# A hand-set order for the five engines of an attention stage, set anew, with 28 changes of array tiling per batch in place of 29

## The chip, the cores and the metric

One Trainium2 chip, one of its cores. The metric is device time in microseconds (us) of one launch, the median of three runs. Times and waits come from one profiled execution of the kernel before. Engines are called as in the profile: PE is TensorE, DVE is VectorE, ACT is ScalarE, POOL is GpSimd, SP is the sync engine, which here only starts DMAs.

## What is computed

The input is 32 sequences (batches) of 256 tokens with 128 features. Two layers are applied, each as `x = x + attention(norm(x)) * silu(ffn(norm(x)))`. Cut to what matters:

```python
x = L0_attn_x                                   # 32 x 256 x 128
xn = _layernorm(x)
s = _L0_attn_ref(xn, ...)                       # a recurrence over the tokens
g = _silu(_L0_ffn_ref(xn, ...))                 # eight experts, one per token
x = x + s * g
xn = _layernorm(x)                              # from here: the last stage
s = _L1_attn_ref(xn, ...)                       # 16 heads of 8, keys in blocks of 64
g = _silu(_L1_ffn_ref(xn, ...))                 # 4 of 16 heads of 64, chosen per batch
return x + s * g
```

`_L1_attn_ref` is a softmax attention whose maximum and correction go block by block over the keys. `_L1_ffn_ref` computes router logits per batch, takes the four best of 16 heads, runs a softmax attention over those and projects the result.

## The kernel before

**Stages.** The first stages (normalization, the recurrence, the experts with their scatter and gather through memory) end at about 398 us. The change is in the last stage alone. It treats one batch at a time, all of its 256 tokens, and is written out without a loop on the chip: `run(eng, step)` calls `step` 36 times (32 batches and four more) for each engine, and a step works on up to five batches at once. `lag(quad, p, k)` gives the batch that came in k steps ago, so `batch0` is the newest and `batch4` the oldest; `runs` leaves a part out where there is no such batch.

```python
            for t in range(B + 4):
                step(t // NQ, t % NQ)
```

**What sets the order.** Nothing but the lines of the five `step` functions. Each engine works through its own list in that order, one instruction after the other. Between engines there are semaphores: `wait_ge(s, n)` waits until s has counted n, `then_inc(s, 1)` counts when an instruction is done, `after(...)` is a wait that is left out while its count is zero or less. A late signal therefore holds back everything that stands behind the waiting instruction on its engine.

**PSUM.** The eight banks are shared out by hand:

```python
        bS, bT = banks[:, 0:1024], banks[:, 1024:2048]
        bC, bA, bF1, bF2 = PS[4], PS[5], PS[6], PS[7]
        bF, bR = (bF1, bF2), (bS, bT)
```

`bS` holds one group of scores at a time, and `bT` one group of shifted scores; both also take the chosen heads' scores (`bR`). `bC` holds P times V, `bA` is used in turn by the transposed input, the logits, both projections and the attention's own output, `bF1` and `bF2` by the chosen heads and the transposed outputs.

**The parts of a batch and their lines** (numbers of the kernel before; those of PE stand 7 higher in the changed kernel, ACT 5, DVE 3, POOL 1).

- PE: `transpose_x` L1858, `logits` L1864, `project_qk` L1869, `project_v` L1876, `transpose_max` L1886, `scores` 0 to 7 L1898, `shifted_scores` 0 to 7 L1912, `values` 0 to 3 L1922, `transpose_o` 0 to 3 L1936, `transpose_attn` L1945, `project_out` L1952, `head_qk` 0 and 1 L1963, `head_v` L1970, `head_scores` 0 and 1 L1983, `head_pt` 0 to 3 L1997, `head_out` 0 and 1 L2005, `routed_out` L2012 and L2014.
- DVE: `ln_stats` L1505, `route_a` L1516 to L1522 (with the heads' indices), `route_b` L1529, `route_c` L1536 and L1542, `qk_rest` L1549, `head_qk` L1557, `block_max` 0 to 7 L1565, `row_max` L1575, `head_max` L1585, `head_pt` L1592, `attn_norm` L1609 to L1616, `final` L1624.
- ACT: `xT_copy` L1696, `qk_copy` L1701, `probs` L1705 and L1706, `gate_exps` L1710, `mT_copy` L1721, `head_qk` L1732, `head_exp` L1747, `head_pt` L1755, `head_ot` L1761, `routed_tanh` L1767, `exp_scores` 0 to 7 L1773, `ot_copy` 0 to 3 L1778, `attnT_copy` L1783.
- POOL: `gather` L1372 and L1376 (two indirect DMAs for the rows of one batch, from batch 2 on), `inverse_std` L1388, `ln_apply` L1394, `minus_top` L1400, `minus_inverse` L1404, `head_biases` L1409, `split` L1417 and L1418, `split_max` L1425 to L1434, `finish` L1442 and L1445, `head_norm` L1451 and L1454.
- SP: `store_max` L1319 writes the row maxima to memory and `load_max` L1324 reads them back as three more rows of `QS`, which `shifted_scores` 0 waits for; `load_qk` L1313, `load_heads` L1335, `store_parts` L1300, `load_biases` L1342, `store_out` L1347.

**Who waits for whom, around the change.** `scores` i waits for `block_max` i-1 (bS), `shifted_scores` i for `exp_scores` i-1 (bT), `values` g for `exp_scores` 2g+1 and for `ot_copy` g-1 (bC). `transpose_o` g waits for `ot_copy` g. `head_scores` 0 waits for the last `block_max` of the batch before. `transpose_x` waits for `ln_apply`, which follows `inverse_std` and DVE's `ln_stats`. `head_v` waits for ACT's `head_qk`, and this for PE's `head_qk` 1. `project_v` waits for `final` (bA).

**Array tiling.** PE uses its 128 x 128 array in four ways: whole; as two row halves (`scores`, `shifted_scores`, `head_scores`, whose two halves fill different banks); as four column quarters (`values`); as two column halves (`head_out`). A change of tiling is a place in PE's order where two neighbours differ in this.

Of the kernel before, what the change touches and what calls it, by code (L numbers as in the profile page):

```python
# [77 lines left out]
NFIRST = 2  # L78
# [1020 lines left out]
def layer_one(nc, first, X, S, slot, ident, ones, mhalf, banks, PS, ys_dram, parts_dram, mrow_dram, l1_w, out_b,  # L1099
# [7 lines left out]
    with ExitStack() as ctx:  # L1107
# [182 lines left out]
        def _(sp):  # L1290
# [59 lines left out]
            def step(quad, p):  # L1350
                batch0, batch1, batch2, batch4 = (lag(quad, p, k) for k in (0, 1, 2, 4))
                run0, run1, run2, run4 = (runs(b[0]) for b in (batch0, batch1, batch2, batch4))
                if run4:
                    store_out(*batch4)
# [5 lines left out]
                if run0:  # L1360
                    load_heads(*batch0)
                    store_parts(*batch0)
                    load_biases(*batch0)
# [5 lines left out]
        def _(pool):  # L1369
# [88 lines left out]
            def step(quad, p):  # L1458
                batch0, batch1, batch2, batch4 = (lag(quad, p, k) for k in (0, 1, 2, 4))
                run0, run1, run2, run4 = (runs(b[0]) for b in (batch0, batch1, batch2, batch4))  # L1460
# [3 lines left out]
                if run1:  # L1464
                    minus_top(*batch1)
                    split(*batch1)
                    minus_inverse(*batch1)
                if run0:
                    if batch0[0] >= NFIRST:
                        gather(*batch0)  # L1470
                if run4:
                    finish(*batch4)
                if run1:
                    head_biases(*batch1)
                if run2:
                    head_norm(*batch2, 2)

# [15 lines left out]
        def _(dve):  # L1493
# [133 lines left out]
            def step(quad, p):  # L1627
# [4 lines left out]
                if run3:  # L1632
                    head_pt(*batch3, 3)
                if run2:
                    block_max(*batch2, 1)
                if run1:
                    route_a(*batch1)

                if run2:
                    block_max(*batch2, 2)  # L1640
                if run4:
                    attn_norm(*batch4, 0)
                if run1:
                    qk_rest(*batch1)
                    route_b(*batch1)

                if run3:
                    routed_gate(*batch3)
                if run2:
                    block_max(*batch2, 3)  # L1650
                if run4:
                    attn_norm(*batch4, 1)
# [3 lines left out]
                if run1:  # L1656
                    route_c(*batch1)
                if run4:
                    final(*batch4)
                if run2:  # L1660
                    block_max(*batch2, 5)
                    block_max(*batch2, 6)

                if run1:
                    head_qk(*batch1)
                if run0:
                    if batch0[0] >= NFIRST:
                        gated(*batch0)
                if run2:
                    block_max(*batch2, 7)  # L1670
# [480 lines left out]
```

## Time and profile before

| what | value |
|---|---|
| median of three runs | 1231.54 us (1230.17 to 1232.34) |
| the profiled execution's own time | 1231.76 us |
| its span, first to last instruction | 1229.9 us |
| PE matmul, busy | 1074.0 us (87%) |
| DVE, ACT, POOL, busy | 967.1, 878.9, 791.0 us (79, 71, 64%) |
| PE's granted clock over the span | 0.938 |
| moved by DMA | 89.20 MB |

How to read it: busy time is the union of an engine's instructions, and in the last stage every engine has idle time in each step. Which wait delays the end is read from PE's and its partners' rows of one step, not from these shares. A row of a timeline gives the start, the duration, the engine, the line, the operation, the tiles written and read, the number of merged instructions, and in brackets the idle time before it and what ended it. Matmul ends are modelled in it, starts are recorded.

### The profile page before, as it was taken

The numbers are of one execution on the slowest core, as the hardware profiler recorded it, in microseconds if no ns is written. First come the engines' busy times: TensorE is split into PE (matmuls) and PEld (weight loads), VectorE is DVE, ScalarE is ACT, GpSimd is POOL, SyncE is SP. The second block draws the span as 40 slices with busy tenths as digits, with TensorE's granted clock in tenths as the row PEclk, the third lists the DMA queues.
The fourth block names the chain that finished last, engine by engine and source line by source line (L and its number), as shares of the span: only waits on it lengthen the run. The fifth ranks groups of instructions, "written<-read, shape, count | busy, mean of one in ns | idle before, by whom it ended". The sixth has DMA issues, their size and how long they took to land.

```text
span 1229.9 us, 29257 instructions
## 1 busy us (share of the span) xinstructions
PE 1074.0 (87%) x8602; PEld 684.8 (56%) x8603; DVE 967.1 (79%) x2160; ACT 878.9 (71%) x2178; POOL 791.0 (64%) x1144
## 2 busy tenths in 40 slices
PE   2666368999996579999999999999999999999985
PEld 2545245676774345565555565555555555556542
DVE  6678989888897378888888778887888887888861
ACT  3555346777775258888888888888888888888873
POOL 4476766666678166766766676676667766776630
PEclk9766679999998599999999999999999999999997
DMA  9511111111111233233323332332233223323310
GB/s 254 166 40 36 35 56 37 50 44 48 43 53 33 55 94 82 65 76 83 92 64 87 80 83 64 93 83 73 65 93 87 70 67 90 90 68 74 89 27 10
DMA packets 148160, 89.20 MB, mean 73 GB/s; under 512 B 73080, under 2 KB 137272, under 8 KB 147768
## 3 DMA queue, kind: packets, MB, share of 16 engines
q1 hardware_dynamic: 143928, 79.01, 24.9%
q0 software_dynamic: 4096, 8.53, 2.4%
q8 instruction: 67, 1.10, 0.4%
q14 instruction: 69, 0.57, 0.2%
HBM read 55.91 MB, written 31.47 MB: 71 GB/s over the span
## 4 chain that ended last, share of the span: by engine, by line
PE 49%; issue 5%; ACT 4%; DVE 4%; DMA 2%; SPq 2%; POOL 1%; DVEq 0%; POOLq 0%
PE PS L1922 8%; PE PS L1912 6%; PE PS L1983 5%; PE PS L1898 5%; PE PS L2005 5%; ACT PT L1773 4%; DVE bm L1565 3%; PE PS L1970 3%; PE PS L1963 3%; PE PS L1997 3%; PE PS L1952 3%; PE PS L1936 2%; PE PS L1869 2%; PE PS L2014 2%; PE PS L1876 1%
## 5 line engine op out<-in xcount | busy, mean ns | idle before, releaser
L1565 DVE TENSOR_REDUCE bm<-PS 128x16 f32<-128x1024 f32 x256 | 312.3, 1220 | 33.8 <-PE PS L1898 26.2
L1773 ACT ACTIVATE PT<-PS 128x1024 f32<-128x1024 f32 x256 | 262.5, 1025 | 25.8 <-PE PS L1912 22.2
L1922 PE MATMUL PS<-PT,rows 128*32 128x256 f32 x2048 | 139.0, 389 | 1.7 <-ACT OT L1778 1.7
L1454 POOL TENSOR_TENSOR Pr<-Pr,linv 128x512 f32<-128x512 f32 x128 | 132.1, 1043 | 5.0
L1747 ACT ACTIVATE Pr<-PS,nmf 128x256 f32<-128x256 f32 x256 | 117.4, 474 | 0.3 <-DVE nmf L1585 0.3
L1585 DVE TENSOR_REDUCE nmf<-PS 128x4 f32<-128x1024 f32 x64 | 78.4, 1225 | 45.7 <-PE PS L1983 45.7
L1912 PE MATMUL PS<-QS,KS 51*128 51x256 bf16 x1024 | 100.3, 274 | 15.5 <-ACT PT L1773 8.4
L1898 PE MATMUL PS<-KS,QS 48*128 48x256 bf16 x1024 | 100.9, 276 | 9.9 <-DVE bm L1565 6.0
L475 POOL DMA_INDIRECT xs_dram<-rows,slot x64 | 65.8, 1028 | 40.2 <-DVEq L699 22.5
L1001 PE MATMUL PS<-S,wmix 128*128 128x256 f32 (+1 forms) x192 | 70.7, 455 | 17.0 <-DVE diff L727 16.3
L1963 PE MATMUL PS<-xT,wsel 128*128 128x256 f32 x256 | 75.0, 417 | 8.7 <-DMA wsel<-in_qkv_w 5.8
L1922 PEld LDWEIGHTS PS<-PT,rows 128*32 128x32 f32 x2048 | 54.9, 110 | 46.6 <-issue 20.5
L1997 PE MATMUL PS<-ident,Pr 128*128 128x128 f32 x512 | 79.5, 278 | 0.0
L1061 PE MATMUL PS<-up,xsT 128*128 x144 | 77.0, 616 | 2.8 <-issue 2.1
L1417 POOL CAST parts<-rest 128x512 bf16<-128x512 f32 x32 | 19.6, 612 | 91.7 <-DVE rest L1549 91.7
L1442 POOL TENSOR_TENSOR s<-s,g 128x256 f32<-128x256 f32 x32 | 23.3, 728 | 79.8 <-DVE s L1624 79.8
L1376 POOL DMA_INDIRECT rows<-ys_dram,rows x60 | 61.7, 1028 | 17.7 <-issue 9.1
L1451 POOL TENSOR_TENSOR linv<-lsum,rows 128x4 f32<-128x4 f32 x64 | 66.5, 1039 | 9.8 <-ACT Pr L1747 9.8
L1912 PEld LDWEIGHTS PS<-QS,KS 51*128 51x128 bf16 x1024 | 34.6, 94 | 68.4 <-ACT PT L1773 56.2
L1778 ACT COPY OT<-PS 128x256 f32<-128x256 f32 x128 | 47.5, 371 | 34.8 <-PE PS L1922 31.4
L1898 PEld LDWEIGHTS PS<-KS,QS 48*128 48x128 bf16 x1024 | 32.4, 94 | 71.7 <-issue 36.3
L1983 PE MATMUL PS<-Kf,Qf 64*128 64x256 f32 x512 | 70.8, 395 | 0.4 <-DVE bm L1565 0.4
(258 smaller groups left out, 2838.3 us busy)
## 6 DMA issues: line engine op xcount, KB each, us to landing
wsel<-in_qkv_w SPq DMA_DIRECT2D x128, 96.0 KB
parts_dram<-parts SPq DMA_DIRECT2D x32, 384.0 KB
QS<-parts_dram SPq DMA_DIRECT2D x64, 96.0 KB
KS<-parts_dram SPq DMA_DIRECT2D x64, 96.0 KB
xs_dram<-zero_t SPq DMA_DIRECT2D x1, 4752.0 KB, 26.6
xs_t<-xs_dram SPq DMA_DIRECT2D x72, 66.0 KB, 1.8
ys_dram<-ys_t SPq DMA_DIRECT2D x72, 64.0 KB, 1.6
QS<-parts_dram SPq DMA_DIRECT2D x64, 64.0 KB
```

The source lines that it names most:

```text
L1061: pe.matmul(psU[q % 2][:, :], xsT[q % 3][:, :], up[:, bass.ds(e * 2 * HID, 2 * HID)], start=True, stop=True).then_inc(s_up, 1)
L1454: pool.tensor_tensor(Pr[i][:, qt, :, :], Pr[i][:, qt, :, :], linv[:, i, qt, :].unsqueeze(2).broadcast_to([P, 2, SEQ]), ALU.mult).then_inc( ...
L1565: dve.tensor_reduce(bm[:, i // 2, :, 2 * (i % 2):2 * (i % 2) + 2, :].rearrange("p q r b -> p r q b"), bS.rearrange("p (r q b k) -> p r q b ...
L1585: dve.tensor_reduce(nmf[:, i, :, :].rearrange("p q j -> p j q"), bR[i].rearrange("p (j q k) -> p j q k", j=2, q=TB), AX.X, ALU.max, negate ...
L1747: last = act.activation(Pr[i][:, qt, j, :], scored[:, j, qt, :], ACT.Exp, bias=nmf[:, i, qt, j:j + 1], accum_out=lsum[:, i, qt, j:j + 1])
L1773: act.activation(PT[i % 4][:, :, :], bT.rearrange("p (r k) -> p r k", r=2), ACT.Exp).then_inc(s_exp, 1)
L1898: last = pe.matmul(bS[:, (j * TB + qt) * SEQ:(j * TB + qt + 1) * SEQ], QS[q][rows, i, qt * P:(qt + 1) * P], KS[q][rows, i, :], start=True, ...
L1912: last = pe.matmul(bT[:, (j * TB + kt) * SEQ:(j * TB + kt + 1) * SEQ], KS[q][rows, i, kt * P:(kt + 1) * P], QS[q][rows, i, :], start=True, ...
L1922: last = pe.matmul(bC[j * VC:(j + 1) * VC, 0:SEQ], V2[q][:, kt, 4 * g + j, :], PT[(2 * g + j // 2) % 4][:, j % 2, kt * SEQ:(kt + 1) * SEQ] ...
L1963: last = pe.matmul(bA[:, k * SEQ:(k + 1) * SEQ], wsel[q % 2][:, k, i * P:(i + 1) * P], xT[q % 2][:, :], start=True, stop=True)
L1983: last = pe.matmul(bR[i][:, (j * TB + qt) * SEQ:(j * TB + qt + 1) * SEQ], Qf[rows, i, qt * P:(qt + 1) * P], Kf[rows, i, :], start=True, st ...
L1997: last = pe.transpose(bF[i][:, at:at + P], Pr[i][:, qt, j, kt * P:(kt + 1) * P], ident[:, :])
```

## The change

The functions that issue instructions stay as they are, and every engine issues the same instructions per batch. The five `step` functions list them in another order, and a step now begins and ends at another place of PE's order, so that several parts have moved by one in their `batch` number. Going round once, PE's new order is: `transpose_x`, `head_pt` 3, `head_scores` 1, `transpose_max`, `head_out` 0, `head_out` 1, `scores` 0, `values` 2, `transpose_o` 0, `transpose_o` 1, `scores` 1, `logits`, `routed_out`, `project_qk`, `values` 3, `scores` 2, `shifted_scores` 0, `transpose_o` 2, `transpose_o` 3, `head_pt` 0, `shifted_scores` 1, `scores` 3, `transpose_attn`, `shifted_scores` 2, `project_out`, `scores` 4, `values` 0, `shifted_scores` 3, `project_v`, `head_pt` 1, `scores` 5, `shifted_scores` 4, `head_qk` 0, `values` 1, `shifted_scores` 5, `scores` 6, `head_qk` 1, `head_pt` 2, `scores` 7, `shifted_scores` 6, `head_v`, `shifted_scores` 7, `head_scores` 0. SP's order, going round, is as it was.

The diff, cut to the parts that are spoken of below:

```diff
@@ POOL @@
+                if run1:
+                    if batch1[0] >= NFIRST:
+                        ln_apply(*batch1)
+                if run3:
+                    split_max(*batch3)
                 if run2:
                     head_norm(*batch2, 0)
                     head_norm(*batch2, 1)
                 if run1:
                     minus_top(*batch1)
-                    split(*batch1)
-                    minus_inverse(*batch1)
                 if run0:
                     if batch0[0] >= NFIRST:
                         gather(*batch0)
+                if run1:
+                    split(*batch1)
+                    minus_inverse(*batch1)
                 if run4:
                     finish(*batch4)
+
+                if run2:
+                    head_norm(*batch2, 2)
                 if run1:
                     head_biases(*batch1)
-                if run2:
-                    head_norm(*batch2, 2)
-
...
                 if run0:
                     if batch0[0] >= NFIRST:
                         inverse_std(*batch0)
-                    if batch0[0] >= NFIRST:
-                        ln_apply(*batch0)
-                if run2:
-                    split_max(*batch2)
@@ DVE @@
...
+                if run2:
+                    block_max(*batch2, 6)
                 if run0:
                     if batch0[0] >= NFIRST:
                         ln_stats(*batch0)
-
+                if run2:
+                    block_max(*batch2, 7)
+                    head_pt(*batch2, 2)
+
+                if run2:
+                    row_max(*batch2)
                 if run1:
                     head_max(*batch1, 0)
                 if run2:
-                    head_pt(*batch2, 2)
-                    row_max(*batch2)
+                    head_pt(*batch2, 3)
                 if run1:
                     head_max(*batch1, 1)
@@ ACT @@
...
+                if run4:
+                    ot_copy(*batch4, 3)
+                if run3:
+                    exp_scores(*batch3, 0)
+                if run1:
+                    probs(*batch1)
                 if run3:
                     exp_scores(*batch3, 1)
...
```

On POOL the gather has moved. The rows are those of one step in the middle of the stage, before and in the change; L1376 and L1377 are the two indirect DMAs.

```order
491 L1400 TENSOR_SCALAR ntop<-top 128x1
492 L1417 CAST parts<-rest 128x2x256
493 L1418 TENSOR_TENSOR parts<-rest,parts 128x512
494 L1404 TENSOR_SCALAR nprob_inv<-prob_inv 128x1
495 L1372 COPY rows<-slot 128x2
496 L1376 DMA rows<-ys_dram,rows 128x128 x2
497 L1442 TENSOR_TENSOR s<-s,g 128x256
```

```order
491 L1401 TENSOR_SCALAR ntop<-top 128x1
492 L1373 COPY rows<-slot 128x2
493 L1377 DMA rows<-ys_dram,rows 128x128 x2
494 L1418 CAST parts<-rest 128x2x256
495 L1419 TENSOR_TENSOR parts<-rest,parts 128x512
496 L1405 TENSOR_SCALAR nprob_inv<-prob_inv 128x1
497 L1443 TENSOR_TENSOR s<-s,g 128x256
```

The gather now follows the router's first product (`minus_top`) at once and no longer waits behind the two halves of `split` and `minus_inverse`.

On ACT the router's exponentials (`probs`) have moved. The rows are from the copy of Q and K out of PSUM (L1701, now L1706) to the first exponentials of shifted scores (L1773, now L1778); L1705 and L1706 are `probs` before, L1710 and L1711 now.

```order
855 L1701 CAST parts<-PS 128x2x256
856 L1705 ACTIVATE prob,prob_sum<-lg,ntop 128x16
857 L1706 ACTIVATE rows<-top,ntop 128x4
858 L1767 ACTIVATE y2t<-PS 128x256
859 L1773 ACTIVATE PT<-PS 128x1024
860 L1778 COPY OT<-PS 128x256
861 L1773 ACTIVATE PT<-PS 128x1024
```

```order
842 L1706 CAST parts<-PS 128x2x256
843 L1783 COPY OT<-PS 128x256
844 L1778 ACTIVATE PT<-PS 128x1024
845 L1710 ACTIVATE prob,prob_sum<-lg,ntop 128x16
846 L1711 ACTIVATE rows<-top,ntop 128x4
847 L1778 ACTIVATE PT<-PS 128x1024
```

They stood ahead of `exp_scores` 0 and now stand between `exp_scores` 0 and 1, and `ot_copy` 3 has gone from between these two to ahead of both.

On PE, the stretch from the logits (L1864, now L1871) to `transpose_attn`'s neighbourhood, in the change alone:

```order
1149 L1871 MATMUL PS<-rows,xsum 128x16
1150 L2019 MATMUL PS<-rows 128x128
1151 L2021 MATMUL PS<-rows,OTf 128x128 x2
1152 L2019 MATMUL PS<-rows 128x128
1154 L1876 MATMUL PS<-xT,rows 128x256 x2
1155 L1929 MATMUL PS<-PT,rows 32x256 x8
1156 L1905 MATMUL PS<-KS,QS 128x256 x4
1157 L1919 MATMUL PS<-QS,KS 128x256 x4
1158 L1943 MATMUL PS<-ident,OT 128x128 x4
1159 L2004 MATMUL PS<-ident,Pr 128x128 x4
1160 L1919 MATMUL PS<-QS,KS 128x256 x4
1162 L1952 MATMUL PS<-ident,attn 128x128 x2
```

`values` 3 (L1929) now comes four parts behind the logits, with `scores` 2, `shifted_scores` 0 and the transposes of the output (L1943) right behind it; before, `shifted_scores` 0 stood ahead of `values` 3.

## Rows read from the trace of the kernel before

**Rows 1.** Window: PE, PEld, DVE, ACT, POOL busy, clock, DMA. Its `scores`: count, busy.

```profile
495.00:1103.00 608.00, 596.49 (x5653) 360.11 (x5651) 495.87 (x1000) 504.69 (x1226) 420.91 (x651) 1.00 0.31 80
...
L1898 PE MATMUL PS<-KS,QS 48*128 48x256 bf16 x800 | 78.2, 274 | 2.5
```

**Rows 2.** Timeline of PE, one step: two score groups in a row, then `values` 3.

```profile
671.94 0.39 PE L1912 MATMUL PS<-QS,KS 51*128 51x256 bf16 x4
672.17 0.38 PE L1898 MATMUL PS<-KS,QS 48*128 48x256 bf16 x4
672.48 1.07 PE L1922 MATMUL PS<-PT,rows 128*32 128x256 f32 x16
```

**Rows 3.** Timeline of PE, the same step: three places where PE stands still.

```profile
666.13 1.07 PE L1922 MATMUL PS<-PT,rows 128*32 128x256 f32 x16
667.30 0.39 PE L1898 MATMUL PS<-KS,QS 48*128 48x256 bf16 x4
...
677.95 0.66 PE L1997 MATMUL PS<-ident,Pr 128*128 128x128 f32 x4
678.77 0.68 PE L1876 MATMUL PS<-rows,xT 128*128 128x128 f32 x4 [0.16 <-DVE s L1624]
...
683.07 1.13 PE L1963 MATMUL PS<-xT,wsel 128*128 128x256 f32 x4
684.26 0.39 PE L1912 MATMUL PS<-QS,KS 51*128 51x256 bf16 x4
```

**Rows 4.** Timeline of PE, the same step: `values` 0 and `project_out`.

```profile
675.76 1.07 PE L1922 MATMUL PS<-PT,rows 128*32 128x256 f32 x16
676.77 0.71 PE L1952 MATMUL PS<-rows,attnT 128*128 128x128 f32 x4
```

**Rows 5.** Timelines of ACT and DVE, the same step: who takes those results up.

```profile
673.62 0.37 ACT L1778 COPY OT<-PS 128x256 f32<-128x256 f32 x1 [0.22 <-PE PS L1922]
...
678.14 0.37 ACT L1778 COPY OT<-PS 128x256 f32<-128x256 f32 x1 [0.97 <-PE PS L1922]
...
678.20 0.42 DVE L1624 TENSOR_TENSOR s<-PS,rows 128x256 f32<-128x256 f32 x1 [1.13 <-PE PS L1952]
```

**Rows 6.** Timelines of DVE and POOL, the same step: the router's first instruction, the gather.

```profile
668.89 0.16 DVE L1516 TENSOR_TENSOR lg<-PS,rows 128x16 f32<-128x16 f32 x1
...
669.36 0.26 POOL L1400 TENSOR_SCALAR ntop<-top 128x1 f32<-128x1 f32 x1 [0.93 <-DVE top L1519]
...
674.45 0.19 POOL L1372 COPY rows<-slot 128x2 int32<-128x2 int32 x1
...
676.32 0.96 POOL L1376 DMA_INDIRECT rows<-ys_dram,rows  x1 [0.30 <-issue]
```

**Rows 7.** Waits of DVE from 560 to 1090 us: us in total, times, longest.

```profile
DVE s L1624 <- PE PS L1952: 21.7, 20, 1.4
```

**Rows 8.** Timeline of ACT, the same step: `probs` to its successor; an exponential and its successor.

```profile
671.42 0.31 ACT L1705 ACTIVATE prob<-lg,ntop 128x16 f32<-128x16 f32 x1
...
672.05 0.38 ACT L1767 ACTIVATE y2t<-PS 128x256 f32<-128x256 f32 x1
...
679.93 1.02 ACT L1773 ACTIVATE PT<-PS 128x1024 f32<-128x1024 f32 x1
680.85 0.41 ACT L1689 ACTIVATE rows<-rows 128x256 f32<-128x256 f32 x1
```

**Rows 9.** Timelines of DVE, POOL and ACT: `ln_stats`, `ln_apply`, the second half of `head_qk`.

```profile
684.28 0.49 DVE L1505 BATCH_NORM_STATS2 rows<-X 128x6 f32<-128x128 f32 x2
...
686.17 1.63 POOL L1394 TENSOR_SCALAR rows<-X,rows 128x128 f32<-128x128 f32 x2
...
684.70 0.56 ACT L1732 ACTIVATE Kf<-PS,gb,gc 128x256 f32<-128x256 f32 x1
```

**Rows 10.** Timeline of DVE, the same step, and waits of PE from 560 to 1090 us.

```profile
680.25 1.23 DVE L1565 TENSOR_REDUCE bm<-PS 128x16 f32<-128x1024 f32 x1 [0.49 <-PE PS L1898]
...
PE PS L1912 <- DMA QS<-mrow_dram: 1.8, 3, 0.8
```

More of the change, by code:

```diff
@@ L1631, in step @@
                     block_max(*batch2, 0)
[L1632 to L1635, printed above, removed]
+                if run4:
+                    attn_norm(*batch4, 0)
                 if run1:
@@ L1651, in step @@
                 if run4:
-                    attn_norm(*batch4, 1)
+                    final(*batch4)
                 if run2:
                     block_max(*batch2, 4)
[L1656 to L1665, printed above, removed]
                 if run0:
@@ L1668, in step @@
                         gated(*batch0)
+                if run1:
+                    route_c(*batch1)
                 if run2:
-                    block_max(*batch2, 7)
+                    block_max(*batch2, 5)
+                if run1:
+                    head_qk(*batch1)
+                if run2:
+                    block_max(*batch2, 6)
                 if run0:
@@ L1804, in step @@
                 if run3:
+                    ot_copy(*batch3, 0)
+                if run3:
                     exp_scores(*batch3, 4)
-                if run0:
-                    if batch0[0] >= NFIRST:
-                        z_tanh(*batch0)
-                if run3:
-                    exp_scores(*batch3, 5)
+                    correction(*batch3)
                 if run2:
@@ L2020, in step @@
                 run0, run1, run2, run3 = (runs(b[0]) for b in (batch0, batch1, batch2, batch3))
+                if run3:
+                    values(*batch3, 1)
+                    shifted_scores(*batch3, 5)
                 if run2:
-                    head_out(*batch2, 0)
+                    scores(*batch2, 6)
                 if run1:
-                    head_scores(*batch1, 1)
+                    head_qk(*batch1, 1)
+                if run2:
+                    head_pt(*batch2, 2)
+                    scores(*batch2, 7)
+                if run3:
+                    shifted_scores(*batch3, 6)
+                if run1:
+                    head_v(*batch1)
+                if run3:
+                    shifted_scores(*batch3, 7)
+                if run1:
+                    head_scores(*batch1, 0)
                 if run0:
@@ L2064, in step @@
                     head_pt(*batch1, 0)
-                    scores(*batch1, 4)
+                if run2:
+                    shifted_scores(*batch2, 1)
+                if run1:
+                    scores(*batch1, 3)
+                if run3:
+                    transpose_attn(*batch3)
                 if run2:
@@ L2069, in step @@
                 if run3:
[L2070 removed]
+                    project_out(*batch3)
+                if run1:
+                    scores(*batch1, 4)
                 if run2:
                     values(*batch2, 0)
[L2073 to L2074 removed]
+                    shifted_scores(*batch2, 3)
+                if run0:
+                    project_v(*batch0)
                 if run1:
+                    head_pt(*batch1, 1)
                     scores(*batch1, 5)
                 if run2:
[L2078 to L2084 removed]
                     shifted_scores(*batch2, 4)
[L2086 to L2087 removed]
                 if run0:
                     head_qk(*batch0, 0)
[L2090 to L2107 removed]
             run(pe, step)
```

127 lines of the change are left out of this document (51 added, 76 removed).

## The prediction

> **What bounds the kernel now.** I read the windows first, then PE's timeline, then those of its partners. In the steady part of the stage PE is busy for 596.49 of 608 us at a granted clock of 1.00, that is at 2.4 GHz; the next engine, ACT, for 504.69 [rows 1]. Each batch has 32 matmul records of `scores`, so 800 are 25 batches, and a step takes 608 / 25 = 24.3 us. The stage is a pipeline paced by PE: an instruction that moves on another engine costs nothing unless PE then stands still. A busy PE hides short waits, since a row's end overlaps the next row's start, so I go by distances between starts. In the step shown they exceed the plain ones at a few places [rows 3]: `scores` 1 comes 1.17 us after `values` 2, where a `values` normally takes 1.01 to its successor [rows 4] (0.16); `project_v` 0.82 after `head_pt` 1, plain 0.49 (0.33), waiting for `final`; `shifted_scores` 7 comes 1.19 after `head_qk` 1, plain 1.06 (0.13). With two of under 0.1 us near `scores` 6, PE stands still for about 0.8 us a step. So 23.5 of 24.3 us are PE's own work, and a perfect order could gain 0.8.
>
> **A late signal.** One of these waits has an odd cause, and it matters here. `values` 3 starts at 672.48 and its modelled end is 673.55 [rows 2]; ACT takes it up at 673.62 [rows 5]. `values` 0 ends at 675.76 + 1.07 = 676.83 [rows 4], but ACT, idle, starts its copy at 678.14, and DVE starts `final` at 678.20 though `project_out` ended at 677.48 [rows 5]. Both results come late together, 1.3 and 0.7 us. Meanwhile POOL issues the gather; its second DMA starts at 676.32 [rows 6]. Matmuls that end in this time are signalled only 1.8 us after that start. DVE's wait there comes in 20 of 22 steps, 1.09 us on average and 1.4 at most against 1.13 in this step [rows 7]: it belongs to the step, not to chance. I take it that PE's signals are held from about the second gather's start until 1.8 us later. Now the victims are lightly loaded; the cost is the 0.33 us before `project_v`.
>
> **The change, part by part.** PE's own work stays, one change of tiling goes. Two score groups of the same tiling start 0.23 apart, and a whole-array or column part follows a score group after 0.31 [rows 2]: **-0.1 us** a step. The Trainium skill, *TensorEngine Tiling (Array Packing)*, Tiling Modes, says that a mode switch drains the array; by the rule too the gain is one drain, and the row prices it at 0.08.
>
> The 0.8 us of waits go: `scores` 1 now has `values` 2 and two transposes between it and `scores` 0, 1.9 us for the 1.7 that `block_max` 0 takes with its signals, where it had 1.54; `project_v` stands behind `values` 0 and `shifted_scores` 3 and no longer just after the held `project_out`; `shifted_scores` 7 has `head_v` ahead of it. **-0.8**.
>
> New waits. (A) `probs` now lies between `exp_scores` 0 and 1 on ACT. From `shifted_scores` 0 to 2 PE has two more transposes, `head_pt` 0, `shifted_scores` 1, `scores` 3 and `transpose_attn` to do: 0.32 + 0.51 + 0.53 + 0.23 + 0.31 + 0.37 = 2.3 us by their distances in this trace. ACT needs 0.44 (a score group of 0.39 and its signal), 0.92 for the exponentials, 0.63 for `probs`, 1.02 for the next exponentials [rows 8] and 0.07 back: 3.1. **+0.8**. (B) `ln_stats` now stands ahead of `block_max` 7, and `transpose_x` waits for its end. From `scores` 6: 0.44, `block_max` 6 with 1.23 less the tenth by which neighbours overlap [rows 10], then 686.17 + 1.63 - 684.28 = 3.52 to the end of `ln_apply` [rows 9], in all 5.15. PE's eight parts between take 4.6. (C) `head_v` needs both of ACT's `head_qk` halves: from PE's `head_qk` 1, 684.70 + 0.56 - 683.07 = 2.2 [rows 3, 9]; PE has 2.05 in between. C lies inside B's path, so B and C together make **+0.5**, not 0.7.
>
> (D) The gather moves ahead of `split` and `minus_inverse`. Count from the logits' start. `transpose_o` 1 ends 0.2 before it, `attn_norm` 0 takes DVE until 0.57, the router's first instruction follows. POOL's `minus_top` comes 0.47 later, the slot copy 0.16 after that, the second gather another 1.87 [rows 6]: 3.07. On PE, `values` 3 ends at 0.24 + 1.12 + 1.06 + 1.07 = 3.5, 0.4 into the hold (`values` 0 fell 0.5 into it before). Its signal comes at 4.87; behind it wait the ACT queue (`ot_copy` 3, then `exp_scores` 0) and with them `transpose_o` 3 on PE, due at 4.2, possible at 5.3. That is +1.1, and A follows after it, since `exp_scores` 0 shifts by the same. Bounds: zero if PE's signals are free, 1.4 if the hold lasts as in the worst step. I take **+0.95**, near the step shown, since some holds will end sooner.
>
> Other moves are covered: `head_biases` behind `head_norm` 2 ends at about the time `head_qk` 0 is ready (a few hundredths if this cover goes); `split`, behind the gather, ends 9 us ahead of `load_qk`'s use; SP keeps its order, and the transposed maxima have some 6.9 us from ACT's copy to `shifted_scores` 0 in place of 5.7. The waits for that transfer, 1.8 us in three of 22 steps [rows 10], should go: **-2 us** once.
>
> Sum per step: -0.1 - 0.8 + 0.8 + 0.5 + 0.95 = +1.35. It counts in some 28 of 31 steps, since the first ones wait for the filling pipeline: +37.8 - 2 = +36. The profiled execution took 1231.8 us, 0.2 over the median; hence **1267 us**.
>
> **Rivals.** (1) *The gather holds nobody back*, and the late results have another cause tied to their place. Then D is nil: +0.4 x 28 - 2 = +9, 1241 us. The steady 1.8 us behind the gather speaks against it; that no row shows a gather at another place, for it. The Trainium skill, *SBUF — State Buffer*, Who interferes with whom, says that PE and ACT never wait on anyone; by that rule there is no D. The rule is about SBUF ports and rows 4 and 5 show late results beside it, so it moves me little. (2) *Faster: the waits are covered.* D and B turn on when POOL gets there. If POOL is late, held up by `head_norm`, the gather starts after `values` 3 has been signalled and D goes; if ACT reaches `probs` before `shifted_scores` 0 is done, A shrinks. It decides from the point where the new waits stay under 0.9 us a step. With A alone left the step gains 0.1, 1229 us; with all gone 0.9 x 28 = 25, 1206 us. For it: 0.8 us of waits surely go. Against it: A is a chain of ACT's own durations and no other engine's haste shortens it. (3) *More waits than counted*, such as PE's granted clock falling, which was 0.938 over the whole span against 1.00 in the steady part. One step in ten at 1.2 GHz would add 3 x 23 = 70 us, over 1300. PE stays over nine tenths busy, so hardly. (4) *The change is not what it says.* The listing shows the same instructions in the new order; nothing is left of this one.
>
> **How the numbers follow.** Forecast (1.2 to 1.45 us a step, 1263 to 1274): 0.66. Rival 1, 1236 to 1246: 0.14. Between these two, a shorter hold: 0.06. Rival 2: 0.10, of which 0.03 within 0.2% and 0.07 faster. Rival 3 and other extra waits: 0.04. A measurement of this kernel can tell about 0.2%, 2.5 us, from no change. Faster 0.07, same 0.03, slower 0.90. Range 1236 to 1278: it takes in rival 1 and the worst hold (0.3 x 28 = 8 more), and leaves out rivals 2 and 3.
>
> **What would show it.** In the profile after: steps of `transpose_x` 25.5 to 25.8 us apart; ACT's `ot_copy` 3 idle for over 1 us behind `values` 3 and starting 1.8 us after the second gather; `shifted_scores` 2 waiting for the exponentials with `probs` between; `transpose_x` just behind `ln_apply`; `final` no longer late. Rival 1 shows 24.6 us and no such wait of ACT. I am wrong altogether if steps are under 24.3.

## The result, and the profile after

The changed kernel takes **1261.56 us** (median of 4 runs, 1260.40 to 1265.16), the kernel before 1231.10 on the same chip: a ratio of 1.0242, with a 95% interval of 1.0223 to 1.0261. It is slower, as forecast, and inside the range; the point forecast of 1267 was 5.4 us too high.

| what | before | after |
|---|---|---|
| the profiled execution's own time | 1231.76 us | 1261.85 us |
| its span | 1229.9 us | 1259.9 us |
| PE's granted clock over the span | 0.938 | 0.931 |
| distance of two `transpose_x`, median of the steady steps | 24.25 us | 25.26 us |
| the same, mean of all 31 | 24.26 us | 25.21 us |

31 x 0.95 = 29.5 of the 30.1 us between the two profiled executions lie in these steps. The window of 608 us and the scores in it, as in [rows 1], in the trace after:

```profile
495.00:1103.00 608.00, 572.44 (x5443) 349.58 (x5442) 488.71 (x967) 479.91 (x1180) 410.22 (x626) 1.00 0.30 77
...
L1905 PE MATMUL PS<-KS,QS 48*128 48x256 bf16 x772 | 75.2, 273 | 0.0
```

The clock is 1.00 in this window as before, so the time isn't the clock's. PE is idle for 35.6 us in place of 11.5, and 24 steps fit in where 25 did. One step in the middle, on PE, from `values` 3 to `shifted_scores` 2 (to be held against [rows 2]), and its end:

```profile
962.30 1.07 PE L1929 MATMUL PS<-PT,rows 128*32 128x256 f32 x16
963.30 0.39 PE L1905 MATMUL PS<-KS,QS 48*128 48x256 bf16 x4
963.53 0.38 PE L1919 MATMUL PS<-QS,KS 51*128 51x256 bf16 x4
963.84 0.44 PE L1943 MATMUL PS<-ident,OT 128*128 128x128 f32 x2
964.96 0.44 PE L1943 MATMUL PS<-ident,OT 128*128 128x128 f32 x2 [0.68 <-ACT OT L1783]
965.24 0.60 PE L2004 MATMUL PS<-ident,Pr 128*128 128x128 f32 x4
965.89 0.39 PE L1919 MATMUL PS<-QS,KS 51*128 51x256 bf16 x4
...
967.40 0.39 PE L1919 MATMUL PS<-QS,KS 51*128 51x256 bf16 x4 [0.39 <-ACT PT L1778]
...
977.78 1.09 PE L1990 MATMUL PS<-Kf,Qf 64*128 64x256 f32 x8
979.04 0.44 PE L1865 MATMUL PS<-ident,rows 128*128 128x128 f32 x2 [0.17 <-POOL rows L1395]
```

The three new waits stand here as they were foretold: `transpose_o` 3 for ACT's `ot_copy`, `shifted_scores` 2 for an exponential, `transpose_x` for `ln_apply`. POOL and ACT in the same step (as [rows 5, 6]):

```profile
963.05 0.95 POOL L1377 DMA_INDIRECT rows<-ys_dram,rows  x1 [0.30 <-issue]
...
964.53 0.37 ACT L1783 COPY OT<-PS 128x256 f32<-128x256 f32 x1 [1.54 <-PE PS L1929]
```

`values` 3 ends at 963.37, ACT is idle and takes it up 1.16 us later, 1.48 after the second DMA of the gather. One step has an irregular gather, an experiment that the chip made by itself. Its second DMA starts 2.06 us behind the first and not 1.41:

```profile
986.91 1.11 POOL L1377 DMA_INDIRECT rows<-ys_dram,rows  x1 [0.32 <-POOL rows L1373]
988.97 0.96 POOL L1377 DMA_INDIRECT rows<-ys_dram,rows  x1 [0.96 <-issue]
...
988.69 0.37 ACT L1783 COPY OT<-PS 128x256 f32<-128x256 f32 x1 [0.44 <-PE PS L1929]
```

`values` 3 ended at 988.63 there, ahead of the second DMA, and ACT starts its copy 0.06 us later. That step took 24.40 us, from 979.04 to 1003.45; its neighbours took 25.26 and 25.27. So 0.86 us of a step are the late signal. This is read from one step; a chip without late signals gives the same step below.

The waits from 560 to 1090 us (us in total, times, longest):

```profile
ACT OT L1783 <- PE PS L1929: 29.0, 21, 1.9
...
DVE s L1627 <- PE PS L1959: 12.7, 21, 0.6
...
PE PS L1943 <- ACT OT L1783: 11.1, 16, 0.8
PE PS L1919 <- ACT PT L1778: 10.4, 25, 0.8
...
PE PS L1865 <- POOL rows L1395: 3.6, 21, 0.2
```

DVE's wait ahead of `final`, 0.6 us on average, is nearly half of that in [rows 7], and PE's waits for the transposed maxima [rows 10] are gone.

### The profile page after: what moved, and what is told of

It is laid out like the page before. It is cut to its first block, busy times and chain, and to the rows that moved or that the text cites. A ratio compares the mean times of both kernels' runs of the same rounds, so it can differ in the third digit from the quotient of the medians.

```text
span 1259.9 us, 29285 instructions
## 1 busy us (share of the span) xinstructions
PE 1077.5 (86%) x8602; PEld 690.6 (55%) x8603; DVE 978.3 (78%) x2160; ACT 870.3 (69%) x2178; POOL 797.3 (63%) x1144
## 3 DMA queue, kind: packets, MB, share of 16 engines
q8 instruction: 68, 1.11, 0.4%
## 4 chain that ended last, share of the span: by engine, by line
PE 29%; POOL 18%; issue 12%; ACT 6%; DVE 2%; SPq 1%; DMA 0%; POOLq 0%; ACTq 0%; DVEq 0%
PE PS L1929 6%; POOL Pr L1455 5%; PE PS L1970 3%; PE PS L1990 3%; PE PS L2012 3%; ACT PT L1778 3%; POOL linv L1452 2%; PE PS L1905 2%; PE PS L1919 2%; POOL rows L1395 2%; ACT Pr L1752 2%; PE PS L2021 1%; PE PS L1977 1%; PE PS L1876 1%; DVE nmf L1588 1%
## 5 line engine op out<-in xcount | busy, mean ns | idle before, releaser
L1778 ACT ACTIVATE PT<-PS 128x1024 f32<-128x1024 f32 x256 | 263.7, 1030 | 49.1 <-PE PS L1919 46.4
L1929 PE MATMUL PS<-PT,rows 128*32 128x256 f32 x2048 | 139.1, 390 | 0.2 <-ACT OT L1783 0.2
L1452 POOL TENSOR_TENSOR linv<-lsum,rows 128x4 f32<-128x4 f32 x64 | 71.7, 1121 | 71.0 <-ACT Pr L1752 71.0
L1929 PEld LDWEIGHTS PS<-PT,rows 128*32 128x32 f32 x2048 | 54.1, 110 | 57.1 <-issue 35.3
L1377 POOL DMA_INDIRECT rows<-ys_dram,rows x60 | 61.8, 1030 | 19.4 <-issue 9.8
L1002 PE MATMUL PS<-S,wmix 128*128 128x255 f32 (+1 forms) x192 | 66.3, 431 | 0.0
```

The costliest lines, as they stand in the source:

```text
L1452: pool.tensor_tensor(linv[:, i, :, :].rearrange("p q j -> p (q j)"), lsum[:, i, :, :].rearrange("p q j -> p (q j)"), minus1[:, :], ALU.pow ...
L1778: act.activation(PT[i % 4][:, :, :], bT.rearrange("p (r k) -> p r k", r=2), ACT.Exp).then_inc(s_exp, 1)
L1929: last = pe.matmul(bC[j * VC:(j + 1) * VC, 0:SEQ], V2[q][:, kt, 4 * g + j, :], PT[(2 * g + j // 2) % 4][:, j % 2, kt * SEQ:(kt + 1) * SEQ] ...
```

## The experiments

The twelve runs fell on four chips, each used in one sitting, and the kernel before does not take the same time on all of them. The ratio beside each result is to the kernel before on the same chip. Late signals are counted in the trace as those of PE's semaphores that come over 0.15 us after the modelled end of their matmul.

| chip | kernel before there | late signals in each trace of this document |
|---|---|---|
| of the result | 1231.1 us | 120 (kernel before), 117 (changed kernel) |
| second | 1221.8 us | 0 in each of four |
| third | 1223.8 us | 0 in each of three |
| fourth | 1230.8 us | 120, 114, 119 (the three runs with halved work), 60 (first try) |
| fifth | 1230.2 us | 17 (second try) |

The first may be the fourth or fifth again; the records don't tell.

### Is it the gather? Second chip

**The changed kernel and the kernel before, each without the gather's two DMAs** (from the third batch on; the experts' rows are then missing from the output):

```diff
-                if run0:
-                    if batch0[0] >= NFIRST:
-                        gather(*batch0)
...
-                act.wait_ge(s_y[q % 2], 32 * n + 32)
+                if t < NFIRST:
+                    act.wait_ge(s_y[q % 2], 32 * n + 32)
```

> The changed kernel without the two indirect DMAs of `gather` in the last stage; ACT's `z_tanh` no longer waits for them, so batches 2 to 31 use the rows of batches 0 and 1 in place of their own. Theory H (the second gather holds back PE's signals): term D goes. One step of the changed kernel had its second gather 0.66 us late and took 24.40 us in place of 25.25; all steps should look like it, ACT's `ot_copy` 3 starting within 0.1 us of the end of `values` 3. 28 x 0.85 = 24 us less: 1238 us (1234 to 1242). Rival P (the signals are late because of something else at that place, such as SP's transfers or PE's own sequence): steps stay at 25.2, 1259 to 1263 us.

> The kernel before without the two indirect DMAs of `gather` in the last stage, otherwise as the run above: batches 2 to 31 use the rows of batches 0 and 1. Theory H: `final` and `ot_copy` 0 start at once behind PE, `project_v` loses its wait of 0.33 us and the later ones move with it; steps 23.8 to 23.95 in place of 24.25: 28 x 0.38 = 11 us less, 1220 us (1216 to 1224). Rival P: 1230 to 1233 us.

Measured: 1235.81 us for the changed one (1.0135, 1.0096 to 1.0175), steps of 24.39; 1221.91 us for the one before (1.0009, 0.9995 to 1.0023), steps of 23.81. Both look like a success of the theory, but the second says at once that something is off: the kernel before with its gather took 1221.77 us on this chip, so taking the gather out gained nothing there. Neither run is evidence for or against the theory; the changed kernel with its gather, on the third chip below, takes the same steps of 24.39 us.

**The kernel before, its gather as early as in the change:**

```diff
                     minus_top(*batch1)
-                    split(*batch1)
-                    minus_inverse(*batch1)
                 if run0:
                     if batch0[0] >= NFIRST:
                         gather(*batch0)
+                if run1:
+                    split(*batch1)
+                    minus_inverse(*batch1)
```

> The kernel before with one part of the change alone: `gather` goes ahead of `split` and `minus_inverse`, right behind `minus_top`. Theory H: the second gather starts 4.6 + 0.16 + 1.87 = 6.6 us behind `transpose_x` and holds until 8.1 to 8.4; `shifted_scores` 0, which ends at 7.5, is signalled 0.6 to 0.9 late, and `exp_scores` 0 and `shifted_scores` 1 come as much later; `project_v` loses its 0.33. Net 0.3 to 0.6 per step more, 1240 to 1249 us. Rival P: the late results stay with `values` 0 and `project_out`, 1230 to 1233 us.

Measured: 1223.46 us (1.0004, 0.9987 to 1.0022), steps of 23.81. Neither expectation was met. The trace shows why: it has the gather, and no late signal. DVE's wait ahead of `final`, 1.09 us on average in [rows 7], is 0.44 here:

```profile
DVE s L1625 <- PE PS L1953: 9.7, 22, 0.4
```

**The changed kernel, its gather back behind `split` and `minus_inverse`** (the same edit turned round).

> The changed kernel with `gather` back behind `minus_inverse`, as it was before. Theory H: `values` 3 is signalled at once (0.85 us a step gained), but the second gather now starts 15 us behind `transpose_x`, its rows land at about 17.4, and ACT's `z_tanh`, ahead of `exp_scores` 3, has to wait for them where it now starts at 15.0: 2.2 us more, with `shifted_scores` 4 behind it. Steps 26.3 to 26.8, 1290 to 1305 us, so that the gather's early place is needed in this order. Rival P: the late signals stay as well, steps over 27, 1315 us or more. If the rows land sooner than that, 1238 us.

Measured: 1332.25 us (1.0901, 1.0877 to 1.0925), steps of 27.8. The two DMAs of the gather now start 12.7 and 14.1 us into the step, and ACT's `z_tanh` waits for its rows with the exponentials behind it:

```profile
605.26 0.42 ACT L1694 ACTIVATE rows<-rows 128x256 f32<-128x256 f32 x1 [2.43 <-DMA rows<-ys_dram,rows]
```

The time is the one that rival P named (over 1315 us), but not for its reason: the trace has no late signal. What the forecast of 1290 to 1305 us left out is PE's granted clock. It falls from 1.00 to half, 1.2 GHz, for 3.4 us or more in most steps here, where PE is busy for 549 of the 608 us of the window of above, and did not in that window before or after the change (596 and 572 us). Two steps in a row, with the clock as the third number from the right:

```profile
616.33:642.57 26.24, 23.72 (x227) 14.44 (x227) 20.75 (x41) 19.93 (x50) 16.85 (x27) 1.00 0.27 74
642.57:670.35 27.78, 25.29 (x226) 14.87 (x227) 20.76 (x41) 19.92 (x50) 16.82 (x27) 0.94 0.28 69
```

Five steps with the clock at 1.00 throughout take 26.24 to 26.27 us, which is the 26.3 that was expected, three more with full clock 26.9 to 27.6, and most of the others about 27.8. So some 1.5 us of the usual step go with the lower clock, and 1.85 (26.24 - 24.39) with the late rows. The run is no evidence on the signals. It shows what the early gather is there for: in this order ACT comes to `z_tanh` some 14 us into the step, when the late gather's second DMA has only just been started.

### The changed kernel itself on another chip. Third chip

> The changed kernel unchanged, on whatever chip this run gets, because the runs with the gather's two DMAs left out came from a chip whose kernel before took 1222 us in place of 1231 and whose trace of the kernel before, with its gather early, showed no late signal of PE. Theory H (PE's results are signalled late behind the gather's second DMA, but only on some chips): where no signal of PE comes over 0.15 us late in this trace, the steps are 24.4 to 24.5 us, the time 1235 to 1238 us and the ratio to the kernel before 1.012 to 1.016; where signals do come late behind the second DMA, the steps are 25.2 to 25.3 us, the time 1258 to 1265 us, the ratio 1.022 to 1.026. Rival P (the late results belong to their place in PE's order and not to the gather, and the 24.4 us of the run without the gather came from lighter memory traffic): steps of 25.2 us and 1258 us or more here too, whatever the signals show.

Measured: 1234.70 us (1.0100, 1.0078 to 1.0122), median steps of 24.39, no late signal. Same program, 27 us less, and just under what the theory gives for a chip without late signals (1235 to 1238 us, ratio 1.012 to 1.016). Its rows for the place of above, on ACT, POOL and PE:

```profile
893.30 0.37 ACT L1783 COPY OT<-PS 128x256 f32<-128x256 f32 x1 [0.45 <-PE PS L1929]
893.82 1.02 ACT L1778 ACTIVATE PT<-PS 128x1024 f32<-128x1024 f32 x1
894.74 0.30 ACT L1710 ACTIVATE prob<-lg,ntop 128x16 f32<-128x16 f32 x1
...
895.34 1.02 ACT L1778 ACTIVATE PT<-PS 128x1024 f32<-128x1024 f32 x1
...
892.92 0.95 POOL L1377 DMA_INDIRECT rows<-ys_dram,rows  x1 [0.30 <-issue]
...
892.17 1.07 PE L1929 MATMUL PS<-PT,rows 128*32 128x256 f32 x16
...
896.42 0.39 PE L1919 MATMUL PS<-QS,KS 51*128 51x256 bf16 x4 [0.41 <-ACT PT L1778]
```

The gather starts at the same point of the step, `values` 3 ends 0.32 us after its second DMA as before, and ACT takes the result up 0.06 us later. It agrees with the irregular step of the first chip to 0.01 us. Rival P as it was put, steps of 25.2 us here too, has fallen. That the late signals follow the gather and not the place in PE's order, this run can't show, since nothing is late in it; for that there are the irregular step above and the run with the gather moved (the first try, below). The Trainium skill, *SBUF — State Buffer*, Who interferes with whom, says "PE and ACT never wait on anyone" of the SBUF ports. Nothing in the rows of these two chips speaks against it; on the others it doesn't cover what the rows show, results that are ready and told late.

**The gather ahead of the first `head_norm`:**

```diff
+                if run0:
+                    if batch0[0] >= NFIRST:
+                        gather(*batch0)
                 if run2:
                     head_norm(*batch2, 0)
                     head_norm(*batch2, 1)
                 if run1:
                     minus_top(*batch1)
-                if run0:
-                    if batch0[0] >= NFIRST:
-                        gather(*batch0)
```

> The changed kernel with the gather ahead of POOL's first two head_norm and of minus_top, so that its second DMA starts some 4 us earlier in the step, at a place where block_max and head_exp alone take results from PE. Theory H on a chip that shows late signals: the 0.9 us at values 3 go, and as much or less comes back at the new place: steps 24.4 to 24.9 us, 1236 to 1250 us. Theory H on a chip without late signals: the same as the changed kernel there, within 2 us. Rival P: the same as the changed kernel on either chip. Note that the gather cannot start before the experts' rows of the batch have their places, which POOL's own earlier work gives, so no new wait is expected.

Measured: 1235.81 us (1.0102, 1.0082 to 1.0121), steps of 24.40, no late signal. It could not tell the theories apart, since the chip had nothing to hold. It shows only that the gather's place is free otherwise.

### What is step A? Third and fourth chip

**`probs` ahead of both exponentials:**

```diff
+                if run1:
+                    probs(*batch1)
                 if run4:
                     ot_copy(*batch4, 3)
                 if run3:
                     exp_scores(*batch3, 0)
-                if run1:
-                    probs(*batch1)
```

> The changed kernel with ACT's probs back ahead of ot_copy 3 and exp_scores 0, all else as changed. The prediction's step A (shifted_scores 2 comes 0.8 us late because probs lies between the two exponentials): most of it goes, 0.6 to 0.7 us in each of some 28 steps, so 17 to 20 us under the changed kernel. Rival (two exponentials in a row with their signals need 3.0 us by themselves against PE's 2.25 us of work between shifted_scores 0 and 2, so that probs sits in a gap of ACT's): at most 0.05 us a step, 0 to 2 us under the changed kernel, shifted_scores 2 still 3.0 us behind shifted_scores 0.

Measured: 1234.36 us (1.0098, 1.0075 to 1.0121) against 1234.70, steps of 24.39. The rival holds. ACT and PE in this run:

```profile
892.16 1.02 ACT L1778 ACTIVATE PT<-PS 128x1024 f32<-128x1024 f32 x1 [0.33 <-PE PS L1919]
893.67 1.02 ACT L1778 ACTIVATE PT<-PS 128x1024 f32<-128x1024 f32 x1 [0.49 <-PE PS L1919]
...
891.72 0.39 PE L1919 MATMUL PS<-QS,KS 51*128 51x256 bf16 x4
...
893.24 0.39 PE L1919 MATMUL PS<-QS,KS 51*128 51x256 bf16 x4
...
894.75 0.39 PE L1919 MATMUL PS<-QS,KS 51*128 51x256 bf16 x4 [0.53 <-ACT PT L1778]
```

With nothing between the exponentials, ACT stands still for 0.49 us, waiting for `shifted_scores` 1. That in turn waits for the first exponential, since the two share `bT`. The chain goes twice round: 894.75 - 891.72 = 3.03 us, as with `probs` in the gap (896.42 - 893.40 = 3.02).

**The first two exponentials halved, then `ln_apply` too, and both cuts in the kernel before:**

```diff
-                act.activation(PT[i % 4][:, :, :], bT.rearrange("p (r k) -> p r k", r=2), ACT.Exp).then_inc(s_exp, 1)
+                h = 1 if i < 2 and t > 0 else 2
+                act.activation(PT[i % 4][:, 0:h, :], bT.rearrange("p (r k) -> p r k", r=2)[:, 0:h, :], ACT.Exp).then_inc(s_exp, 1)
...
-                for j in range(TB):
+                for j in range(TB if t < 6 else 1):
```

> The changed kernel with exp_scores 0 and 1 taken over 512 of their 1024 columns (from the second batch on), so that each takes some 0.43 us less of ACT; it leaves half of the exponentials of two score groups out. Theory E (step A is real, but its cause is the chain shifted_scores 0, exponential, shifted_scores 1, exponential, shifted_scores 2 and not probs): without late signals PE waits in this chain for 0.17 us ahead of shifted_scores 1 and 0.47 ahead of shifted_scores 2, and with a chain that is 0.86 us shorter both go, but probs may now lie in the way of the second exponential for 0.1 to 0.2. Steps of 23.9 to 24.1 us against 24.39, 8 to 13 us under the changed kernel. Rival W (the waits only move on: what is gained at shifted_scores 2 is lost at the next of ACT's results or at transpose_x): steps over 24.3 us, at most 3 us gained.

> As the run with halved exponentials, and in ln_apply only the first of its two instructions (from the seventh batch on), which leaves half of a batch's normalized rows out. Theory: steps B and C are real beside A; transpose_x comes 0.29 us later behind head_scores 0 than plain in the changed kernel, waiting for ln_apply, and ln_apply is now 0.8 us shorter. A further 0.2 to 0.3 us a step, so steps of 23.6 to 23.8 us, 16 to 21 us under the changed kernel and about the kernel before; what is left over PE's own 23.1 is head_v's 0.2 and waits that come up anew. Rival: B was only the echo of A (the whole step shifts together), nothing more is gained over the run with the exponentials alone.

> The kernel before with the same two cuts (exponentials 0 and 1 halved, ln_apply's second instruction left out). Control: the kernel before has neither of these chains on PE's path; theory: at most 0.05 us a step, within 3 us of the kernel before. If it gains 8 us or more, the cuts measure less work in general and not these chains.

Measured on the fourth chip, which has late signals, so that steps are to be held against the 25.26 of the result: 1252.76 us, steps of 24.95; 1243.81 us, 24.74; the kernel before with both cuts 1229.66 us (0.9999, 0.9984 to 1.0014), steps of 24.19 for 24.25. The first cut gains 0.3 us a step, 8.8 us in all if the changed kernel takes 1261.6 there too (that pair of kernels was measured on the first chip; the kernel before agrees to 0.3 us). The second gains 0.21 a step, in some 25 steps, and 9.0 us more, of which the steps explain 5; the intervals of the two ratios (1.0153 to 1.0209, 1.0085 to 1.0142) leave room for that. The control gains nothing that can be told, so the cuts measure these chains and not less work in general. The first gained less than the 0.6 it freed ahead of `shifted_scores` 1 and 2 (0.13 and 0.47), because other waits came up behind it; PE in that run (this kernel's numbers are one higher):

```profile
911.96 0.44 PE L1953 MATMUL PS<-ident,attn 128*128 128x128 f32 x2 [0.18 <-DVE attn L1619]
912.33 0.39 PE L1920 MATMUL PS<-QS,KS 51*128 51x256 bf16 x4
912.86 0.71 PE L1960 MATMUL PS<-rows,attnT 128*128 128x128 f32 x4
```

`shifted_scores` 2 now follows `transpose_attn` without a wait, but `transpose_attn` waits for DVE, and `project_out` comes 0.53 behind `shifted_scores` 2 in place of 0.33 (967.40 to 967.73 in the trace after): ACT reaches `attnT_copy` later than PE reaches its consumer.

### An order to beat both. Fourth and fifth chip

**First try**, the kernel before with parts of each engine's list moved. On POOL:

```diff
+gather b0
 head_norm0 b2
...
 minus_inverse b1
-gather b0
+head_norm2 b2
+head_biases b1
 finish b4
-head_biases b1
-head_norm2 b2
```

> The kernel before with another order of its parts, meant to beat both: on PE head_scores 1 stands ahead of head_out 0, project_qk ahead of scores 2, head_pt 2 ahead of shifted_scores 7, shifted_scores 3 ahead of scores 5 and project_v ahead of head_pt 1, on ACT probs and ot_copy 2 come later, and the gather stands first in POOL's step, so that late signals, where there are any, fall on a place where nobody waits. By the distances of PE's parts from the traces so far, about 0.3 us of PE's waits and changes of tiling go: steps of 23.55 to 23.7 us against 23.81 on a chip without late signals, 3 to 7 us under the kernel before; 12 to 18 us under it on a chip with late signals. Rival: what each engine waits for is only displaced, and the steps stay at 23.8 us or more.

Measured: 1232.29 us (1.0029, 1.0005 to 1.0053), steps of 24.35 at the median. The rival was right: it is no faster than the kernel before. Two rows of its waits name the culprit:

```profile
POOL gb L1409 <- DMA bsel<-in_qkv_b: 61.2, 21, 3.8
...
PE PS L1898 <- DMA KS<-parts_dram: 10.1, 16, 1.5
```

`head_biases` waits 2.9 us a step for a DMA, `finish` stands behind it, SP's `store_out` waits for `finish`, `load_qk` stands behind `store_out`, and `scores` 0 gets its K rows late. The run has a use all the same: the gather lies elsewhere in the step, and the late signals have moved with it. POOL, PE and DVE in one step:

```profile
887.32 0.96 POOL L1376 DMA_INDIRECT rows<-ys_dram,rows  x1 [0.31 <-issue]
...
888.15 0.39 PE L1864 MATMUL PS<-rows,xsum 128*128 128x16 f32 x2
...
888.82 0.17 DVE L1519 TENSOR_TENSOR lg<-PS,rows 128x16 f32<-128x16 f32 x1 [0.55 <-PE PS L1864]
```

`logits` ends at 888.54 and DVE, idle, takes it up 0.28 later, 1.50 after the second DMA. `values` 2, which ends 0.9 us after that DMA in this step, is signalled at the same time; over the steps it is 0.84 to 0.92 late where it ends 0.6 after the DMA. So on a chip with late signals they follow the gather: other results of PE are late now than in the kernel before, and all of them end behind the second DMA.

**Second try**, `finish` ahead of `head_biases` again, the gather first on POOL, and PE's order from the kernel before with these moves (ACT and DVE to fit):

```diff
-head_out0 b2
 head_scores1 b1
 transpose_x b0
+head_out0 b2
 head_pt3 b2
+transpose_max b2
 scores0 b1
-transpose_max b2
+transpose_o0 b3
+logits b0
+transpose_o1 b3
 values2 b3
 scores1 b1
-logits b0
-transpose_o0 b3
-transpose_o1 b3
 head_out1 b2
+project_qk b0
 scores2 b1
-project_qk b0
...
+shifted_scores3 b2
 scores5 b1
-shifted_scores3 b2
...
 head_qk1 b0
+head_pt2 b1
 shifted_scores7 b2
...
 head_v b0
-head_pt2 b1
```

> A second order meant to beat both kernels, after the first one failed because POOL's head_biases, which waits for a DMA, stood ahead of finish, and so store_out, load_qk and scores 0 came late. Here finish stands ahead of head_norm 3 and head_biases again; the gather still stands first in POOL's step; on PE head_pt 2 follows head_qk 1, project_qk stands ahead of scores 2, shifted_scores 3 ahead of scores 5, transpose_o 0 and 1 ahead of values 2, and ACT's attnT_copy, ot_copy 1 and ot_copy 2 are moved to fit. By PE's distances in the traces so far a step should take 23.6 to 23.8 us: on a chip with late signals 0.45 to 0.65 us less than the kernel before, 10 to 18 us under it (ratio 0.985 to 0.992); on a chip without them 0 to 0.2 us less, 0 to 6 us under it (0.995 to 1.0). Rival: the K rows of the next batch come too late again, because split now waits behind more work of POOL, and PE waits at scores 0 as in the first such order: steps over 24 us, no gain or a loss.

Measured: 1220.72 us (0.9927, 0.9907 to 0.9948), steps of 24.03. It beats the kernel before by 9.5 us, just under the 10 to 18 expected; the changed kernel wasn't run on this chip and took 1235 us at best elsewhere. The gain is that of late signals avoided: its steps are 0.22 us shorter than the kernel before's with late signals (24.25) and 0.22 longer than that kernel's without (23.81). On a chip without late signals it wasn't run; by these steps, an estimate, it would lose there. 3 late signals are left in this stage, 14 lie ahead of it: hardly a result of PE ends between about 0.55 and 1.5 us after the second DMA. The step misses its 23.8 at one new wait of PE:

```profile
897.23 0.38 PE L1912 MATMUL PS<-QS,KS 51*128 51x256 bf16 x4
897.86 1.13 PE L1963 MATMUL PS<-xT,wsel 128*128 128x256 f32 x4 [0.24 <-DVE Kf L1560]
```

## Why the prediction was right, and where it wasn't

Its sum of +1.35 us a step measured +1.01, and it was right in sign and mechanism with one cause mistaken. That its size came out was in part luck: the changed kernel takes 1235 us, 10.9 over the kernel before, where signals aren't late, and nothing in the one trace that the prediction had could tell which kind of chip the result would come from. With the traces without late signals (steps of 23.81 and 24.39) the terms come apart:

- **Own work, -0.1:** undersized. Leaving out the waits, the distances of a step sum to 23.35 before and 23.12 after, so -0.23. Two places make it. `head_out` 0 and 1 side by side take 1.88 where each took 1.01 alone (0.14); this is the change of tiling that went. `routed_out` takes 1.11 to a whole-array neighbour and 1.21 to a score group (0.10), and the change that stood behind it now stands between `project_qk` and `values`, where `project_qk` takes 0.96 against 0.97 before, to a whole-array neighbour: it costs nothing there. The same large parts pay elsewhere: `head_qk` 1 now takes 0.97 and not 1.06, but `head_v` 1.06 and not 0.97. Behind `values` a change follows in every trace and takes 1.00 whatever it is, so its price can't be read. The prediction counted changes at 0.08 each instead of reading each distance.
- **Old waits, -0.8:** right, a little low. Before, 24.25 - 23.35 = 0.90; of this the late signals are 24.25 - 23.81 = 0.44 (forecast 0.33). All went. The prediction took one of the waits near `scores` 6 for under 0.1. In the step shown, `shifted_scores` 4 comes 0.73 behind `project_v`, 0.06 after the end of an exponential; the same pair takes 0.54 in the second try, where the exponential is long done:

```profile
678.41 1.03 ACT L1773 ACTIVATE PT<-PS 128x1024 f32<-128x1024 f32 x1
...
679.50 0.39 PE L1912 MATMUL PS<-QS,KS 51*128 51x256 bf16 x4
```

```profile
893.39 0.61 PE L1876 MATMUL PS<-rows,xT 128*128 128x128 f32 x4
893.93 0.39 PE L1912 MATMUL PS<-QS,KS 51*128 51x256 bf16 x4
```

- **(A), +0.8:** about right in size, wrong in cause. PE waits 0.17 ahead of `shifted_scores` 1 and 0.47 ahead of `shifted_scores` 2, 0.64. The prediction charged `probs` with it. The run with `probs` moved away gained nothing (1234.36 against 1234.70 us). What the prediction's chain left out is that the second exponential also waits for `shifted_scores` 1, and this for the first exponential; that leaves ACT a gap of 0.49 us, in which `probs` fits.
- **(B, C), +0.5:** right, though its terms add to 5.09 and not 5.15. `transpose_x` comes 0.29 late, `head_v` 0.21. The halved `ln_apply` gave 0.21 back. A wait of 0.13 ahead of `transpose_attn` was not foreseen. A to C with it make 1.27 where 1.3 was forecast.
- **(D), +0.95:** right on the chip of the result, 25.26 - 24.40 = 0.86; the second DMA started 3.07 us behind the logits' start, as forecast, and the hold ended 1.4 to 1.7 us after it in most steps and not 1.8, which is its median before. On the third chip D is nil and the change costs 1.0%, 10.9 us; the sign stays.
- **Steps and DMA waits:** 28 x 1.35 - 2 = +36 was forecast. All 31 steps together grew by 29.5; PE's waits for `mrow_dram` went as foretold.

-0.23 - 0.90 + 1.27 + 0.86 = +1.00. What the prediction said would be seen was seen, except the 25.5 to 25.8 us between steps and the 1.8 us from the second DMA to `ot_copy` 3, which were 25.26 and 1.48. Rival 1's forecast of about +9 us is what the third chip gives, but not its reason: no trace shows late results with a cause tied to their place. Rival 2 named a real exception, a gather after the signal of `values` 3; it occurred in one step, by 0.65 us of delay in one DMA. Rivals 3 and 4 did not occur.

Not tried: the halved exponentials on a chip without late signals, and, on one with them, the early `head_norm` gather and either kernel without its gather, which would be the plainest test of D. That the gather holds the signals is read from when they come in seven traces, from the irregular step and from the first try. Nor do the runs tell what in the gather does it, POOL's issuing or the transfer behind it.

## What to carry to other kernels

Before charging a wait to the instruction that was put in, walk the whole loop of buffers round it: here the loop of bank, exponential and bank was already longer than PE's work, and `probs` fitted in its gap. Price a change of tiling at the distance of its own two neighbours, since here one was worth 0.14 us, others 0.09 or 0.10, and one nothing. And an indirect DMA issued on POOL belongs where no one waits on PE's results for the next 2 us, in case signals are late; DMA-fed waits (`head_biases`) belong behind what another queue waits for.

## What the runs showed that was not expected

On some chips results of PE are told to the other engines up to 1.5 us late around POOL's indirect DMAs: in the last stage those that end some 0.3 to 1.7 us after the start of the second of a pair, nearly all released 1.4 to 2.1 us after that start (a few already after 0.7), and in the first stages, where eight such DMAs follow each other, by up to 3.7 us. The first of the pair holds nothing: results that end 0.2 to 1.2 us after its start are signalled within 0.02 us. PE itself works on. This goes with the chip or with the sitting, which the runs can't tell apart: the changed kernel has over 100 late signals in this stage on one chip and none on another. Without late signals the kernel before takes 1222 to 1224 us and the changed one 1235; with them 1230 to 1231 and 1262. What sets these chips apart is open; no run here could look at it. For a comparison of two orders it means that the ratio itself changes, here between 1.010 and 1.024, so both must run on the same chip, and on more than one.
